# First cross-attention of a six-block chain: the output product computed from rounded parts and rests, and moved behind the eighth scores of the next tile

## The reference, cut to what matters

```python
def _L0_xattn_ref(latents, context, ln_l_w, ln_l_b, ln_c_w, ln_c_b, Wq, Wkv, Wo, bo):
    ...                                    # H = 16 heads, D = 64, INNER = 1024
    lat = layernorm(latents, ln_l_w, ln_l_b)
    ctx = layernorm(context, ln_c_w, ln_c_b)
    q = (lat @ Wq).reshape(b, n, H, D).transpose(0, 2, 1, 3)
    kv = ctx @ Wkv
    ...
    attn = jnp.einsum('bhnd,bhsd->bhns', q, k) * scale
    attn = jax.nn.softmax(jnp.clip(attn, -11.0, 11.0), axis=-1)
    out = jnp.einsum('bhns,bhsd->bhnd', attn, v)
    out = out.transpose(0, 2, 1, 3).reshape(b, n, INNER)
    return out @ Wo + bo                   # (128 rows x 1024) @ (1024 x 256) per tile
...
x = x + _L0_xattn_ref(_layernorm(x), ctx_1024, ...)
```

## Time and profile before

| | |
|---|---|
| time, three runs | 1001.87 us median (1000.32 to 1002.91) |
| the profiled execution | 1002.35 us, of which 1000.6 us lie between the first and the last instruction |
| PE busy | 953.0 us (95% of the span) |
| PE weight loads busy | 818.4 us (82%), beside the products |
| DVE busy | 612.9 us (61%) |
| ACT busy | 446.0 us (45%) |
| POOL busy | 169.0 us (17%) |
| chain that ended last | PE 82%, DVE 9%, ACT 5%, issue 2%, DMA 1% |
| mean granted TensorE clock | 0.986 |

### The profile page before, as it was taken

How to read it: one execution, slowest core, us unless ns; L and a number is a source line. 1 busy time by engine, 2 the same in 40 slices (tenths; PEclk the granted TensorE clock), 3 DMA queues, 4 the chain that set the end, 5 groups by cost and what they waited for, 6 DMA issues and landing times.

```text
span 1000.6 us, 25932 instructions
## 1 busy us (share of the span) xinstructions
PE 953.0 (95%) x10693; PEld 818.4 (82%) x10693; DVE 612.9 (61%) x1448; ACT 446.0 (45%) x893; POOL 169.0 (17%) x357
## 2 busy tenths in 40 slices
PE   5999999999999989999989999997999999999998
PEld 4788888888888777887779999995888887877887
DVE  5655754654532655667798787776787863554242
ACT  3333332333332466654236666653444343673241
POOL 2312212112012212334310000013112000110000
PEclk9999999999999999999999999997999999999999
DMA  9443142132110292000059999962312002000000
GB/s 323 129 106 75 33 106 74 33 85 52 35 40 4 80 382 85 3 12 24 23 157 343 377 356 360 307 131 46 54 35 44 3 3 75 3 2 1 11 11 22
DMA packets 158612, 101.16 MB, mean 101 GB/s; under 512 B 102104, under 2 KB 148128, under 8 KB 157984
## 3 DMA queue, kind: packets, MB, share of 16 engines
q1 hardware_dynamic: 156960, 95.31, 31.9%
q0 software_dynamic: 1536, 4.20, 1.3%
HBM read 82.96 MB, written 16.52 MB: 99 GB/s over the span
## 4 chain that ended last, share of the span: by engine, by line
PE 82%; DVE 9%; ACT 5%; issue 2%; DMA 1%; POOL 0%; SPq 0%; DVEq 0%; ACTq 0%; POOLq 0%
PE ps L642 9%; PE ps L657 8%; PE ps L2374 8%; PE ps L2387 6%; PE ps L2710 6%; PE ps L674 3%; PE ps L1488 3%; PE ps L1195 3%; PE ps L596 3%; PE ps L693 2%; PE ps L1585 2%; PE ps L626 2%; PE ps L1120 2%; PE ps L1527 2%; PE ps L1130 2%; PE ps L1569 2%
## 5 line engine op out<-in xcount | busy, mean ns | idle before, releaser
L2374 PE MATMUL ps<-moe_xT,ew 128*128 128x128 f32 x736 | 89.5, 275 | 0.9 <-issue 0.8
L785 ACT ACTIVATE x0pT<-ps 128x512 f32<-128x512 f32 x64 | 38.2, 598 | 110.9 <-PE ps L657 110.9
L2374 PEld LDWEIGHTS ps<-moe_xT,ew 128*128 128x128 f32 x736 | 85.8, 192 | 1.7 <-issue 1.4
L1029 POOL TENSOR_SCALAR x0pT<-x0pT 128x512 f32<-128x512 f32 x64 | 40.3, 630 | 188.1 <-ACT x0pT L785 187.1
L2710 PE MATMUL ps<-f,ffw 128*128 128x512 f32 x256 | 60.7, 398 | 0.8 <-issue 0.6
L2710 PEld LDWEIGHTS ps<-f,ffw 128*128 128x128 f32 x256 | 48.9, 192 | 12.0 <-issue 0.9
L2387 PE MATMUL ps<-ew_2hi,eh_hi 128*128 128x256 f32 x184 | 55.5, 301 | 3.2 <-DVE eh_lo L2513 2.8
L642 PE MATMUL ps<-x0wv_hi,x0cT_hi 128*128 128x512 f32 x128 | 53.2, 416 | 4.2 <-DVE x0A_lo L915 4.2
L2323 DVE TENSOR_TENSOR ew_2lo<-ew,ew_2hi 128x1024 fp32r<-128x1024 f32 x46 | 55.9, 1216 | 0.0
L2570 POOL DMA_INDIRECT yg<-moe_out,slot x16 | 16.3, 1017 | 232.2 <-DMA moe_out<-moe_y 162.1
L657 PE MATMUL ps<-x0A_hi,x0cT_hi 128*128 128x512 f32 x128 | 52.0, 406 | 2.5 <-ACT x0pT L785 2.5
(11 more groups left out here) (337 smaller groups left out, 2428.7 us busy)
## 6 DMA issues: line engine op xcount, KB each, us to landing
ew<-L_ffn_W_dram SPq DMA_DIRECT2D x46, 1024.0 KB, 7.7
x0cin<-ctx_dram SPq DMA_DIRECT2D x8, 512.0 KB, 4.7
x1cin<-ctx_dram SPq DMA_DIRECT2D x64, 64.0 KB
x0cn_rows<-x0cn SPq DMA_DIRECT2D x7, 512.0 KB, 2.8
x0cn_blocks<-x0cn_rows SPq DMA_DIRECT2D x56, 64.0 KB, 2.4
x0att_rows<-x0att SPq DMA_DIRECT2D x14, 256.0 KB, 2.5
x0att_blocks<-x0att_rows SPq DMA_DIRECT2D x56, 64.0 KB, 2.6
moe_out<-moe_y SPq DMA_DIRECT2D x23, 128.0 KB, 4.3
```

The source lines that it names most:

```text
L785: nc.scalar.activation(g.pT[:, u, :], ps[:, S_BANK[u % 2], :], ACT.Exp, scale=64.0 ** -0.5).then_inc(C0.exp, 1)
L1029: nc.gpsimd.tensor_scalar(g.pT[:, u, :], g.pT[:, u, :], high, low, ALU.min, ALU.max).then_inc(C0.clip, 1)
L2374: last = nc.tensor.matmul(ps[:, n % 3, j * BT:j * BT + BT], ew1[b % NW][:, i, f * P:f * P + P], xT[b % 2][:, i, :], start=(i == 0), stop=( ...
```

## The change

The output product of the first block is computed from parts as well. ACT rounds x0wo once into x0wo_hi (`wo_upper`, four pieces in tile 0) and each tile's turned x0attT into x0attT_hi (`attT_upper`, two pieces, after the sixth exponentials of the next tile). DVE takes the rests in place (`wo_lower`, `attT_lower`). PE then makes 24 products hi*hi, hi*lo, lo*hi of 128x128 by 128x256 instead of eight full ones. The product of tile t - 1 moves from behind the fourth scores of tile t to behind the eighth, and that of tile 6 (T - 2) to the seam, behind the first `fill_hT`. DVE's `turn_att` moves behind the split of the next context, its `residual` behind the last value copy; that of tile 6 goes to the seam. For the last tile, the two turned halves are each rounded by ACT and their rest taken by DVE.

x0wo_hi takes the place of w_sq[0], whose four loads (256 KB each) move from the start to behind the seam, and x0attT_hi the upper half of padneg, which POOL clears again behind the seam. Semaphore counts follow.

```diff
@@ -171,13 +172,19 @@
             att = sb("x0att", [P, 8, P])
+            attT_at = at[0]
             attT = sb("x0attT", [P, 8, P])
+            attT_lo = nc.alloc_sbuf_tensor_at("x0attT_lo", [P, 8, P], F32R, offset=attT_at)
             wq = sb("x0wq", [P, KD, INNER])
...
             wv_hi = sb("x0wv_hi", [P, KD, INNER], F32R)
+            wo_at = at[0]
             wo = sb("x0wo", [P, 8, D])
+            wo_lo = nc.alloc_sbuf_tensor_at("x0wo_lo", [P, 8, D], F32R, offset=wo_at)
+            wo_hi = nc.alloc_sbuf_tensor_at("x0wo_hi", [P, 8, D], F32R, offset=w_sq_at)
+            attT_hi = nc.alloc_sbuf_tensor_at("x0attT_hi", [P, 8, P], F32R, offset=padneg_at + B * S)
             ln_st = sb("ln_st", [P, 5, 6])
...
@@ -502,12 +509,12 @@
             FILLS += [(("x0", t), f"v{i}") for i in range(2, 4)]
-            FILLS += [(("x0", t - 1), "y")] * (t > 0) + [(("x0", t + 1), "lat")] * nxt
-            FILLS += [(("x0", t), f"v{i}") for i in range(4, 8)]
+            FILLS += [(("x0", t + 1), "lat")] * nxt
+            FILLS += [(("x0", t), f"v{i}") for i in range(4, 8)] + [(("x0", t - 1), "y")] * (0 < t < T - 1)
             if nxt:
...
             else:
-                FILLS += [(0, "hT"), (("x0", t), "T0"), (0, "lat"), (0, "rope"), (0, "qkc"), (0, "v"), (("x0", t), "T1"), (1, "hT"),
+                FILLS += [(0, "hT"), (("x0", t - 1), "y"), (("x0", t), "T0"), (0, "lat"), (0, "rope"), (0, "qkc"), (0, "v"), (("x0", t), "T1"), (1, "hT"),
                           (("x0", t), "y"), (1, "lat"), (1, "qkc"), (1, "rope"), (2, "hT"), (("x0", t), "y2"), (1, "v")]
...
@@ -684,22 +691,24 @@
+            def out_products(t, what, ks):
+                for k in ks:
+                    for n, (m, w) in enumerate(((g.attT_hi, g.wo_hi), (g.attT_hi, g.wo_lo), (g.attT_lo, g.wo_hi))):
+                        last = nc.tensor.matmul(bank_of(t, what)[:, 0:D], m[:, k, :], w[:, k, :], start=(k == ks[0] and n == 0), stop=(k == ks[-1] and n == 2))
+                last.then_inc(C0.fill, 1)
+
             def fill_y(t):
                 if t == 0:
-                    pe.wait_ge(ld["x0o"], 16)
-                pe.wait_ge(C0.attT, 2 * t + 2)
+                    pe.wait_ge(C0.w_lo, KD + 4)
+                pe.wait_ge(C0.attT, 4 * t + 4)
                 wait_bank(pe, t, "y")
-                for k in range(8):
-                    last = nc.tensor.matmul(bank_of(t, "y")[:, 0:D], g.attT[:, k, :], g.wo[:, k, :], start=(k == 0), stop=(k == 7))
-                last.then_inc(C0.fill, 1)
+                out_products(t, "y", range(8))
...
                 wait_bank(pe, t, what)
-                for k in range(4):
-                    last = nc.tensor.matmul(bank_of(t, what)[:, 0:D], g.attT[:, 4 * half + k, :], g.wo[:, 4 * half + k, :], start=(k == 0), stop=(k == 3))
-                last.then_inc(C0.fill, 1)
+                out_products(t, what, range(4 * half, 4 * half + 4))
...
@@ -722,8 +731,6 @@
                     scores(t, i)
-                if t > 0:
-                    fill_y(t - 1)
                 if nxt:
...
                     scores(t, i)
+                if 0 < t < T - 1:
+                    fill_y(t - 1)
                 if nxt:
...
@@ -784,9 +793,21 @@
-            def attT(t):
-                wait_filled(act, t, "T0")
-                nc.scalar.activation(g.attT[:, 0:4, :], bank_of(t, "T0"), ACT.Copy).then_inc(C0.by_act, 1)
+            def attT_upper(t):
+                act.wait_ge(C0.attT, 4 * t + 2)
+                if t > 0:
+                    wait_filled(act, t - 1, "y")
+                for pg in range(2):
+                    nc.scalar.activation(g.attT_hi[:, 4 * pg:4 * pg + 4, :], g.attT[:, 4 * pg:4 * pg + 4, :], ACT.Copy).then_inc(C0.attT_hi, 1)
+
+            def attT_upper_last(pg):
+                wait_filled(act, T - 1, f"T{pg}")
+                nc.scalar.activation(g.attT_hi[:, 4 * pg:4 * pg + 4, :], bank_of(T - 1, f"T{pg}").rearrange("p (c n) -> p c n", c=4), ACT.Copy).then_inc(C0.attT_hi, 1)
+
+            def wo_upper(i):
+                if i == 0:
+                    act.wait_ge(ld["x0o"], 16)
+                nc.scalar.activation(g.wo_hi[:, 2 * i:2 * i + 2, :], g.wo[:, 2 * i:2 * i + 2, :], ACT.Copy).then_inc(C0.w_hi, 1)
...
@@ -815,9 +836,17 @@
                 exp(t, 5)
+                if t > 0:
+                    attT_upper(t - 1)
+                if t == 0:
+                    wo_upper(0)
+                    wo_upper(1)
                 v(t, 6)
...
                 exp(t, 7)
+                if t == 0:
+                    wo_upper(2)
+                    wo_upper(3)
                 if nxt:
...
@@ -938,9 +967,20 @@
-            def attT(t):
-                wait_filled(dve, t, "T1")
-                nc.vector.tensor_copy(g.attT[:, 4:8, :], bank_of(t, "T1")).then_inc(C0.by_dve, 1)
+            def attT_lower(t, pg):
+                dve.wait_ge(C0.attT_hi, 2 * t + pg + 1)
+                half = slice(4 * pg, 4 * pg + 4)
+                nc.vector.tensor_tensor(g.attT_lo[:, half, :], g.attT[:, half, :], g.attT_hi[:, half, :].bitcast(F32), ALU.subtract).then_inc(C0.attT, 1)
+
+            def attT_lower_last(pg):
+                dve.wait_ge(C0.attT_hi, 2 * T - 1 + pg)
+                half = slice(4 * pg, 4 * pg + 4)
+                nc.vector.tensor_tensor(g.attT_lo[:, half, :], bank_of(T - 1, f"T{pg}").rearrange("p (c n) -> p c n", c=4),
+                                        g.attT_hi[:, half, :].bitcast(F32), ALU.subtract).then_inc(C0.by_dve, 1)
+
+            def wo_lower(i):
+                dve.wait_ge(C0.w_hi, KD + i + 1)
+                nc.vector.tensor_tensor(g.wo_lo[:, 2 * i:2 * i + 2, :], g.wo[:, 2 * i:2 * i + 2, :], g.wo_hi[:, 2 * i:2 * i + 2, :].bitcast(F32), ALU.subtract).then_inc(C0.w_lo, 1)
...
@@ -991,25 +1031,36 @@
                 if t > 0:
-                    turn_att(t - 1, 0)
-                    turn_att(t - 1, 1)
                     v(t, 3)
...
                     cT_split(t + 1)
-                if t > 0:
-                    residual(t - 1)
                 if more:
                     norm(t + 2, 1)
+                if t > 0:
+                    turn_att(t - 1, 0)
+                    turn_att(t - 1, 1)
                 v(t, 5)
...
                     norm(t + 2, 2)
+                if t > 0:
+                    attT_lower(t - 1, 0)
+                    attT_lower(t - 1, 1)
                 v(t, 7)
+                if 0 < t < T - 1:
+                    residual(t - 1)
                 if more:
                     norm(t + 2, 3)
+                if t == 0:
+                    wo_lower(0)
+                    wo_lower(1)
                 attend(t, 0)
...
                     q(t + 1)
+                if t == 0:
+                    wo_lower(2)
+                    wo_lower(3)
+                if nxt:
                     A_lower(t + 1, 0)
...
@@ -1713,6 +1764,8 @@
                     continue
+                if n == LEAD - 2:
+                    pe.wait_ge(ld["sq0"], 64)
                 if is_mla(n + 2):
...
@@ -1855,17 +1908,18 @@
                 hT(lo)
-                last(T - 1)
+                last(0)
                 lat(lo)
...
                 rope(lo)
+                last(1)
                 hT(lo + 1)
...
             else:
-                act.wait_ge(pool_setup, 9)
+                act.wait_ge(pool_setup, 10)
                 x1_neg, x1_attT, x1_exps = last
...
@@ -2005,11 +2059,13 @@
                 x0_attend, x0_attT, x0_add_y, x0_residual = last
+                x0_residual(T - 2)
+                x0_attT(0)
                 rotate(lo)
...
                 norm(lo + 1)
-                x0_attT(T - 1)
+                x0_attT(1)
                 norm(lo + 2)
...
@@ -2810,14 +2866,12 @@
             whole(wg[:, :, 0:E], weight("L0_ffn_Wg"), ld["wg"])
-            for i, w in enumerate(("Wq", "Wk", "Wv", "Wo")):
-                whole(w_sq[0][:, :, i, :], weight("L0_ffn_" + w), ld["sq0"])
             def turn_rows(t):
...
                 if t > 1:
-                    sp.wait_ge(C0.turned, t - 1)
+                    sp.wait_ge(C0.turned, 2 * t - 3)
                 blocks = cn_dram.rearrange("(m j) (k q i) -> q k j m i", j=32, k=KD, i=32)
...
@@ -2846,9 +2900,11 @@
             sp.wait_ge(C0.x_done, T)
+            for i, w in enumerate(("Wq", "Wk", "Wv", "Wo")):
+                whole(w_sq[0][:, :, i, :], weight("L0_ffn_" + w), ld["sq0"])
             for i, w in enumerate("QKVO"):
                 whole(w_sq[1][:, :, i, :], weight("L1_attn_W_" + w), ld["sq1"])
-            sp.wait_ge(pool_setup, 8)
+            sp.wait_ge(pool_setup, 9)
             whole(b2[0:E, :], a["L0_ffn_b2"], ld["b2"])
...
@@ -2938,6 +2994,7 @@
             pool.wait_ge(C0.x_done, T)
+            nc.gpsimd.memset(padneg[:, B // 2:B, :], 0.0).then_inc(pool_setup, 1)
             nc.gpsimd.memset(b2[:, :], 0.0).then_inc(pool_setup, 1)
...
```

(19 more changed lines are left out.)

8 lines of the change are left out of this document (4 added, 4 removed).

## The result

| | before | after |
|---|---|---|
| time, 12 runs each, same chip | 1001.47 us median (999.88 to 1007.58) | 996.41 us median (991.23 to 1000.88) |
| the profiled execution | 1002.35 us (span 1000.6) | 996.74 us (span 995.0) |
| mean granted TensorE clock | 0.986 | 0.986 |

The ratio of the times is 0.994, with a 95% interval of 0.9918 to 0.9962: faster by 5.1 us, which is more than the 0.3% that can be told from no change. The forecast was 996.5.

What follows compares the result with a forecast made beforehand. PE's own work was taken to bound tiles 1 to 7. Gains of 4.13 (products), 0.60 (halves) and 0.69 (tile 1's stall) sum to 5.4 us, giving 996.5 us from the median; own range 995.3 to 998.5, 8-in-10 range 994.8 to 999.6.

Steps and rivals of the forecast that it cites:

- The product: Output product of tiles 0 to 6 on PE: 2.87 us for 3.46, gaining 0.59 each, 4.13 us together.
- The halves: Last tile's two half products on PE: 1.43 us each for 1.73, gaining 0.60 us together.
- The stall of tile 1: Tile 1's extra 0.69 us, from the product waiting for late attention rows, goes away.
- Changes of kind, banks, SP: PE's switches between product kinds (upper bound 0.57 us), bank waits and SP's moved weight loads: all cost nothing.
- The seam up to T0: Behind the first block's tiles: tile 6's product moves behind hT and costs nothing extra.
- POOL beside DVE: In the seam, POOL's clearing moves its additions' meeting with a tiny DVE operation: 0, bounds -0.9 and +0.9 us.
- the rival that the meeting dissolves: In the seam, POOL's additions come after DVE's tiny operation: 0.9 us more gain, 995.6 us; chance 0.13.
- DVE's slack: In each tile, DVE has 1.5 us to spare behind the output product before the A rests slip; cost nothing.
- DVE becomes late in every tile: Rival: DVE's work behind the product outlasts its cover, deciding over 4.6 us; at 6.1 us, 1005.5 us; chance 0.06.
- One of the prediction's own signs of being wrong: Forecast wrong if the seam from eighth scores to first FFN product is not shorter by the halves' 0.6 us.
- half of it is given back: Rival: product begins at 3.07 us, kind changes cost 0.57, seam 0.5 to 1; 999.3 us; chance 0.19.
- Weight loads bind: Rival: each load takes its recorded 0.19 us alone, a product 4.56 us; 1010.0 us; chance 0.02.

Runs made afterwards that it cites:

- two kernels: Changed kernel plus two or five unused DVE reductions behind the residual in tiles 1 to 6: 999.02 us (one run) and 1012.65 us median.
- the kernel with the three edits: Changed kernel with POOL held back in the seam, second value product ahead of fill_A 2 and 3, and tile 0's context scaling and wo rests later: 987.99 us median.

## Why the prediction was right

The forecast was 996.5 us, the median 996.41; the gain was 5.1 us for a forecast of 5.4, and the profiled executions differ by 5.6. That the median was hit within 0.1 us is luck: the interval of the ratio alone leaves the gain between 3.8 and 8.2 us. By its own steps:

- **The product.** Forecast 24 x 0.1195 = 2.87 us; measured 2.83, 0.118 each. Seven of them gain 4.4 for 4.13. That the length is the cause is shown by the full product in the new place, which is back at 3.46 and 38.76 a tile. By the 107 ns of a load of 128 columns in the Trainium skill (TensorE: Matmul & The Clock Gate, section "LDWEIGHTS (loading the stationary operand)") 24 products would take 2.56 us, as an estimate; the trace doesn't agree, 2.83 is a tenth more, and the pitch of the earlier trace rows was the better guide.
- **The halves.** Forecast 2 x 0.30; measured 1.73 - 1.42 = 0.31 each.
- **The stall of tile 1.** Forecast 0.69; tile 1 is now 38.13 us, as the others. The parts in the old place show what it would have become, 2.63 us.
- **ACT.** Forecast: roundings hidden by 1.7 us. Measured: two in 1.14 us, and the copy of v6 ends at 121.91, 2.0 ahead of `values` at 123.92.
- **Changes of kind, banks, SP.** Put at nothing, and nothing shows: the product follows the scores and q follows it in the same instant, and PE's idle time in a tile is 0.51 us as before.
- **The seam up to T0.** The step said that y(6) "costs nothing extra". It does more: it stands in a hole where PE had waited for hT. The hole was on the chain of before, between the eighth scores and `fill_lat` of the second block, and I had not looked there. Worth 0.38 against the kernel before, 0.2 by the kernel that moves the product alone.
- **POOL beside DVE.** The step set "what it gives or takes" at 0 with bounds of 0.9 either way; measured -0.77: 0.23 and 0.48 us in `sa_neg` and `h`, and 0.06 behind them. The argument against the rival that the meeting dissolves, "the norm behind it may meet them instead", is what happened: `h` is that norm. I had seen one DVE operation beside the additions and missed the second, 0.65 us right behind it. What I had not done was to lay the 1.8 us of clearing and the additions over DVE's own times: the clearing begins 0.9 us behind the last residual's end (338.96 for 338.02), ends inside the first `sa_neg`, and moves the additions onto `h`. With POOL held back all of it goes, and the 0.9 us that the rival priced with it.
- **DVE's slack.** The step "The slack is 1.5 us before the A rests slip" failed. The 0.5 ahead of q's copy was right (0.62), the 1.02 behind it was not slack, because the copy itself releases the bank and the q piece that `fill_A`'s second group needs. The slack is 0.8 us (two kernels). The price of the residual, norm step and `attend` was right, 3.0 for 3.1, so the wrong slack cost the forecast nothing. But the rival "DVE becomes late in every tile" decides at 3.0 + 0.8 = 3.8 us, not at 4.6, and its price is right from there: each us beyond is one us a tile.

One of the prediction's own signs of being wrong did show: the seam from the eighth scores to the first use of w_sq[0] was to be shorter by the 0.6 us of the halves. It went from 48.49 us (324.75 to 373.24) to 53.57 (317.93 to 371.50), and without the product that moved in, 2.83, that is 2.2 longer. About 2.3 of it is the stretch around 355:363 at the lower clock, which the kernel before did not have there; up to `fill_lat` at 349.52 before and 345.44 after, the seam is 0.1 shorter, because the 0.91 behind the halves eats most of what they and the hole give. Nor does the lower end of the forecast's own range follow from its bounds: half of the POOL bound is 0.45 us, which gives 996.0 and not 995.3.

So the sum came out for the right main reason, the length of the product, the halves and the stall of tile 1. The seam terms that were not forecast, +0.38 and -0.91, have opposite signs, and the seven products gained 0.3 more than forecast; that what is left is only 0.2 us is luck as well. Of the rivals, "half of it is given back" fell: neither 3.07 for the product nor the changes of kind came. "Weight loads bind" fell by the pitch.

What stays open: whether the lower clock at 355:363 has to do with the change (the kernel after has it in both of its profiled executions, the kernel before not; of the ten variants two have it and eight do not), and how the gain of 5.1 divides in the medians, which hold several runs with the lower-clock stretches in other places; the division above is of one pair of executions.

## What to carry to other kernels

Price a product by the pitch of the same form in its own kernel, and then ask what must be ready for it: the same 24 products gained 5.1 us behind the eighth scores and lost 4.7 behind the fourth. Idle time behind a copy is slack only if nobody waits for the copy: before counting it, look for the bank that the copy empties. And when work is added to another engine, lay it and what it pushes back over the small operations that its neighbours have on the chain at that moment.

## What the runs showed of the hardware

Some operations of DVE stretch beside POOL's work. `sa_neg` (128x16) takes 0.17 us with POOL still, 0.62 and 0.65 beside additions, and 0.85 where it starts beside a clearing of 128x2048; `h` (128x256) takes 0.41 with POOL still and 0.88 beside additions. Both read SBUF. Operations that read PSUM did not stretch there: `sa_max` took 1.23 and 1.22 us with and without the clearing beside it, and the four pieces of `rope` (128x128) 1.11 beside the additions in the kernel before and after, 1.13 beside the clearing in the kernel with POOL held back. That the source and not the size decides is what these rows suggest; no run tests it.

The granted clock fell to its lower level behind idle times of PE in tile 0 (2.49 us), in the old place (2.63 us) and at the seam (3.2 us). Where PE was kept busy, in the kernel with the three edits over 110:300 and in the one with tile 0 reordered over 40:50, it stayed at 1.00; over 110:300 so it did in the kernel after, whose PE is idle for 0.51 us a tile. But it also fell at 355:363 in the kernel after and not in the kernel before, though PE's longest idle time in the ten us ahead of it was 0.65 us (345 to 355) and the kernel before has such ones there too (0.66); that stays open.
